# Keys and values of the second attention leave the first attention's loop; keys are repeated by transfers; the first expert group is routed beside group 2's transfers

## What is computed

```python
x = x + tanh(g_xattn[0]) * attention0(layernorm(x), ctx)   # one head, softmax(q ctx^T) ctx
x = x + tanh(g_ffn[0])   * moe0(layernorm(x))              # 16 experts, top 4, one shared expert
x = x + tanh(g_xattn[1]) * attention1(layernorm(x), ctx)   # 16 heads of 8, k = ctx Wk^T + bk, v = ctx Wv^T + bv
x = x + tanh(g_ffn[1])   * moe1(layernorm(x))              # 8 experts, top 2
# attention1:
q = query_states @ Wq.T + bq
k = key_value_states @ Wk.T + bk
v = key_value_states @ Wv.T + bv
attn = softmax(einsum('bhqd,bhkd->bhqk', q * SCALE, k))
out = einsum('bhqk,bhkd->bhqd', attn, v) @ Wo.T + bo
```

## Time and profile before

| | |
|---|---|
| time, median of 3 runs | 337.23 us (336.18 to 338.31) |
| profiled execution | 339.97 us, of which the span is 337.3 us |
| PE busy | 296.4 us (88% of the span), weight loads 222.8 us |
| DVE busy | 247.9 us (73%) |
| ACT, POOL busy | 165.1 us (49%), 103.8 us (31%) |
| mean granted TensorE clock | 0.969 of 2.4 GHz |
| chain that ended last | PE 54%, DVE 17%, ACT 8%, DMA 7%, issue 6% |

### The profile page before, as it was taken

One profiled execution on the slowest core, in us unless ns is written; L12 is line 12 of the kernel. 1 busy time (PEld: TensorE's weight loads), 2 busy tenths in 40 slices (PEclk: granted clock), 3 DMA queues, 4 the chain that ended last, 5 costly groups with the idle time before them and its releaser, 6 DMA issues.

```text
span 337.3 us, 5717 instructions
## 1 busy us (share of the span) xinstructions
PE 296.4 (88%) x1488; PEld 222.8 (66%) x1488; DVE 247.9 (73%) x727; ACT 165.1 (49%) x427; POOL 103.8 (31%) x157
## 2 busy tenths in 40 slices
PE   1889879998998999858898898898887999999995
PEld 1677756665766666537787787787874667676662
DVE  2479778976887977654868868868868877958662
ACT  1237653224233242466798797797862233233321
POOL 6216615020055010263529829829401010100000
PEclk9999958999899999987999999999999999999999
DMA  7901104818605125000000000000004233061550
GB/s 216 328 16 38 31 4 153 247 28 256 166 26 176 54 97 157 0 1 0 2 1 3 2 0 0 0 0 1 3 17 154 83 121 116 22 209 36 165 179 31
DMA packets 16279, 26.45 MB, mean 78 GB/s; under 512 B 2789, under 2 KB 5299, under 8 KB 16051
## 3 DMA queue, kind: packets, MB, share of 16 engines
q1 hardware_dynamic: 15448, 24.93, 24.0%
q10 hardware_dynamic: 808, 1.25, 1.3%
HBM read 24.29 MB, written 1.25 MB: 76 GB/s over the span
## 4 chain that ended last, share of the span: by engine, by line
PE 54%; DVE 17%; ACT 8%; DMA 7%; issue 6%; SPq 3%; POOL 2%; DVEq 1%; ACTq 0%; POOLq 0%
PE bank L547 20%; PE Ybank L569 13%; DMA CR<-comb_rows 4%; PE bank L722 4%; ACT PX L977 3%; DVE cmx L1327 2%; DVE xn L1088 2%; PE Tb L471 2%; DMA comb_rows<-ct 2%; DVE st L1074 2%; SPq L295 1%; DMA CB<-in_consts 1%; DVE recT L1343 1%; SPq L302 1%; DVE xl L1094 1%
## 5 line engine op out<-in xcount | busy, mean ns | idle before, releaser
L890 ACT ACTIVATE sg<-bank 128x512 f32<-128x512 f32 x64 | 38.1, 597 | 76.6 <-PE bank L547 59.4
L334 POOL TENSOR_TENSOR rstd<-ve,mhalf 128x4 f32<-128x4 f32 x16 | 16.2, 1011 | 162.2 <-DVE ve L1081 162.2
L1227 DVE TENSOR_TENSOR hb<-sg,CR 128x512 f32<-128x512 f32 x64 | 44.9, 703 | 18.4 <-DMA CR<-comb_rows 8.4
L1220 DVE TENSOR_TENSOR sg<-sg,bank 128x512 f32<-128x512 f32 x64 | 43.5, 680 | 6.7 <-PE bank L547 4.2
L1327 DVE TENSOR_REDUCE cmx<-bank 128x4 f32<-128x308 f32 x64 | 28.3, 472 | 17.5 <-PE bank L695 17.2
L342 POOL TENSOR_TENSOR KS<-kr,CB 128x1232 fp32r<-128x1232 f32 x16 | 36.1, 2260 | 11.3 <-PE bank L695 11.3
L547 PE MATMUL bank<-xh,WBH 128*128 128x512 f32 x68 | 36.2, 533 | 1.2 <-DVE sg L1220 0.6
L547 PE MATMUL bank<-xh,UPH 128*128 128x512 f32 x64 | 36.2, 566 | 0.0
L569 PE MATMUL Ybank<-hb,W2T 128*128 128x512 f32 x64 | 33.5, 604 | 3.1 <-DVE hb L1227 3.1
L569 PE MATMUL Ybank<-hb,downw 128*128 128x512 f32 x64 | 33.0, 599 | 0.4 <-DVE hb L1227 0.3
L977 ACT ACTIVATE PX<-bank,cmx 128x77 f32<-128x77 f32 x128 | 29.4, 355 | 0.0
(11 more groups left out here) (179 smaller groups left out, 612.0 us busy)
## 6 DMA issues: line engine op xcount, KB each, us to landing
CR<-comb_rows SPq DMA_DIRECT2D x64, 128.0 KB, 3.0
CR<-comb_rows SPq DMA_DIRECT2D x32, 256.0 KB, 3.4
VX<-in_vs_seed SPq DMA_DIRECT2D x4, 320.0 KB, 4.6
w13raw<-in_w SPq DMA_DIRECT2D x1, 1088.0 KB, 11.6
X<-in_x SPq DMA_DIRECT2D x4, 256.0 KB, 9.5
upraw<-in_up SPq DMA_DIRECT2D x4, 256.0 KB, 4.7
out_x<-X SPq DMA_DIRECT2D x4, 256.0 KB, 3.6
cT<-in_ctxT SPq DMA_DIRECT2D x4, 154.0 KB, 6.1
```

Source lines behind the costliest of these rows:

```text
L334: nc.gpsimd.tensor_tensor(rstd[:], ve[:], mhalf[:], ALU.pow).then_inc(rstd_rdy, 1)
L890: A(sg[:, k % 2, :], Gb[k % 2][:], ACT.Silu).then_inc(m.s_done, 1)
L1220: V.tensor_tensor(sg[:, k % 2, :], sg[:, k % 2, :], Ub[k % 2][:], ALU.mult).then_inc(m.t2, 1)
L1227: V.tensor_tensor(hb[:, k % 2, :], sg[:, k % 2, :], CR[:, k % RING, :], ALU.mult).then_inc(m.h_done, 1)
```

## The change

- Stage A: no key work, no value work, no `RK`. Norms 1 to 5 have buffers of their own (`mvA`, `rstdA` and so on), and ACT applies three of them (new `norm_apply` on ACT, four instructions each); the sum of probabilities comes from ACT's exponentials. `W4` and `CN` are loaded by SP.
- Between stage A and unit 0: values (PE, then ACT), keys (PE, `keys_hi` on ACT, `keys_lo` on DVE) for all four groups. The value bias goes through the output projection into `tgbo`.
- The repeating of the keys is done by 16 transfers, `kh` and `kl` to `kr`. They and the 24 value pieces are issued by `later_load`, three behind each unit from unit 14 to unit 27.
- The routing of group 0 is written to DRAM before SP waits for the end of stage A. Each group's routing is one transfer instead of four.
- POOL: `expand_keys` and `place_values(0)` stand behind the splits of `up` and ahead of norm 9.

The core of the diff:

```diff
-            sp.wait_ge(vs_zero, 1)
-            sp.wait_ge(v_done, NG)
-            for h, c, row, key, n in pieces:
-                sp.dma_start(VS[row:row + n, c, h % UH - chunk_head(c)], Vn[key:key + n, h]).then_inc(in_vs, 16)
+            def place_keys(n):
+                a, s = n // NHG, n % NHG
+                src = kh if a < 2 else kl
+                sp.dma_start(kr[32 * a:32 * (a + 1), s, :], src[32 * s:32 * (s + 1), :].bitcast(F32)).then_inc(in_kr, 16)
+
+            def place_values(n):
+                h, c, row, key, rows = pieces[n]
+                sp.dma_start(VS[row:row + rows, c, h % UH - chunk_head(c)], Vn[key:key + rows, h]).then_inc(in_vs, 16)
...
+                first, per = 10, 3
+                if n == first:
+                    sp.wait_ge(k_l, NG)
+                    sp.wait_ge(vs_zero, 1)
+                    sp.wait_ge(v_done, NG)
+                for i in range(per * (n - first), per * (n - first) + per):
+                    if 0 <= i < NHG * 4:
+                        place_keys(i)
+                    elif 0 <= i - NHG * 4 < len(pieces):
+                        place_values(i - NHG * 4)
...
-                for t in range(GB):
-                    sp.dma_start(at[0:m.E, t * P:(t + 1) * P], ct[32 * t:32 * t + m.E, :]).then_inc(rows_out, 16)
-                sp.wait_ge(rows_out, 16 * GB * (m.route_base + g + 1))
+                sp.dma_start(at[0:m.E, :].rearrange("e (t n) -> t e n", t=GB), ct[0:GB * m.E, :]).then_inc(rows_out, 16)
+                sp.wait_ge(rows_out, 16 * (m.route_base + g + 1))
+                if m is mB and g == 0:
+                    sp.wait_ge(a_pv, START + NG)
...
-            sp.wait_ge(a_pv, START + NG)
...
-            pool.wait_ge(d_set, 1)
-            pool.wait_ge(kr_done, START + NG * NHG)
-            expand_keys(0, 0, first=True)
-            expand_keys(1, 1, first=True)
             inv_std(NG + 3)
-            pool.wait_ge(in_seed, 64)
-            pool.wait_ge(in_vs, 16 * len(pieces))
-            place_values(0, 0, first=True)
             inv_std(NG + 4)
             pool.wait_ge(in_up, 96)
             for n in range(NG):
                 split_up(n)
+            pool.wait_ge(in_kr, 16 * NHG * 4)
+            expand_keys(0, 0, first=True)
+            expand_keys(1, 1, first=True)
+            pool.wait_ge(in_seed, 64)
+            pool.wait_ge(in_vs, 16 * len(pieces))
+            place_values(0, 0, first=True)
+            pool.wait_ge(bo_rdy, 1)
             inv_std(2 * NG + 1)
...
+            a_probs_T(2)
+            a_turn(5)
+            a_mix(2)
+            m_logits(mB, 0)
+            a_probs_T(3)
+            a_mix(3)
+
+            setup_values(0)
+            pe.wait_ge(a_exp, NG)
+            setup_values(1)
+            m_route_T(mB, 0)
+            setup_values(2)
+            setup_values(3)
+            pe.wait_ge(v_done, 1)
+            setup_keys(0)
+            pe.wait_ge(v_done, 2)
+            setup_keys(1)
...
+            m = mB
+            m_up(m, 0, 0, ring=False)
+            pe.wait_ge(x_done, START + NG)
+            setup_keys(2)
...
             m_up(m, 0, 1, ring=False)
-            pe.wait_ge(x_done, START + NG)
+            pe.wait_ge(k_l, 2)
+            setup_keys(3)
+            pe.wait_ge(k_l, NG)
             m_body(m, 0, (NG + 2, m, 1))
```

More of the change, by code:

```diff
@@ L263, in load_x, with load_cT @@
                 sp.dma_start(X[:, g * GT:(g + 1) * GT], x[:, g * GT:(g + 1) * GT]).then_inc(in_x[g], 16)
+            def load_cT(half):
+                cols = slice(half * 2 * GS, (half + 1) * 2 * GS)
+                sp.dma_start(cT[:, cols], ctxT[:, cols]).then_inc(in_ct[half], 16)
             load_x(0)
[L266 to L269, removed]
+            load_x(1)
@@ L846, in norm_hi, with norm_apply @@
                 A(dst, Tb[:], ACT.Copy).then_inc(xh_rdy, 1)
-            norm_hi(2, xf[:])
+            def norm_apply(n, g):
+                par = n % 2
+                act.wait_ge(rstdA_rdy, n)
+                act.wait_ge(xnT, n - 1)
+                for t in range(GB):
+                    i = A(xn[:, t * P:(t + 1) * P], X[:, g * GT + t * P:g * GT + (t + 1) * P], ACT.Identity,
+                          bias=shiftA[:, par, t:t + 1], scale=rstdA[:, par, t:t + 1])
+                i.then_inc(xn_rdy, 1)
             def a_exps(g):
@@ L940, in m_body @@
                         m_route_copy(nxt[1], nxt[2])
+            norm_hi(1, xf[:, 0])
+            act.wait_ge(in_w, 16)
+            A(WQH[:], W4[:, 0, :], ACT.Copy).then_inc(su_a, 1)
+            norm_hi(2, xf[:, 1])
             a_exps(0)
+            norm_apply(3, 2)
             a_probs(0)
-            with act.Fori(0, NG - 2) as g:
-                a_body(g, xf[:], True)
-            a_body(NG - 2, xh[:, 0:GT], True)
-            a_body(NG - 1, None, False)
+            norm_hi(3, xf[:, 0])
+            a_exps(1)
+            norm_apply(4, 3)
+            a_probs(1)
+            norm_hi(4, xf[:, 1])
+            a_exps(2)
+            norm_apply(5, 0)
+            a_probs(2)
+            norm_hi(5, xh[:, 0:GT])
+            a_exps(3)
+            m_route_act(mB, 0)
+            a_probs(3)
+            values(0)
+            values(1)
+            m_route_copy(mB, 0, first=True)
+            values(2)
+            values(3)
+            keys_hi(0)
+            keys_hi(1)
             m = mB
             m_silu(m, 0, 0)
+            keys_hi(2)
             m_silu(m, 0, 1)
+            keys_hi(3)
             m_body(m, 0, (NG + 2, m, 1), begun=2)
@@ L1105, in _, with norm_statsA @@
-            dve.wait_ge(in_x[0], 16)
-            norm_stats(1, 0)
-            norm_apply(1, 0, first=True)
-            dve.wait_ge(in_x[1], 16)
-            norm_stats(2, 1)
-            dve.wait_ge(in_small, 16)
-            values(0)
-            norm_apply(2, 1)
+            def norm_statsA(n, g):
+                par = n % 2
+                if n > 2:
+                    dve.wait_ge(xn_rdy, n - 2)
+                for t in range(GB):
+                    i = V.bn_stats(st[:, t, :], xt(g, t))
+                i.then_inc(statsA, 1)
+                wait_apart(dve, statsA, n)
+                for t in range(GB):
+                    i = V.bn_aggr(mvA[:, par, t, :], st[:, t, :])
+                i.then_inc(aggrA, 1)
+                wait_apart(dve, aggrA, n)
+                if n > 2:
+                    dve.wait_ge(rstdA_rdy, n - 2)
+                V.tensor_scalar(veA[:, par], mvA[:, par, :, 1], EPS, None, ALU.add)
+                V.tensor_scalar(lessA[:, par], mvA[:, par, :, 0], -1.0, None, ALU.mult).then_inc(varA, 1)
@@ L1292, in _ @@
             i.then_inc(gw_hi, 1)
-            dve.wait_ge(in_x[3], 16)
-            with dve.Fori(0, NG - 3) as g:
-                a_body(g, g + 2, True, g + 3)
+            a_update(0)
             dve.wait_ge(x_done, START + 1)
-            a_body(NG - 3, NG - 1, True, 0)
-            a_body(NG - 2, 0, True)
-            norm_lo(NG + 1, 0)
-            a_body(NG - 1, None, False)
+            norm_statsA(5, 0)
+            a_share(1)
+            a_maxima(2)
+            a_update(1)
+            a_share(2)
+            a_maxima(3)
+            dve.wait_ge(bv_mm, 1)
+            V.scalar_tensor_tensor(out=tgbo, in0=tgbo, scalar=tg[:, 1:2], in1=bank[0][:, 0:P], op0=ALU.mult,
+                                   op1=ALU.add).then_inc(bo_rdy, 1)
+            norm_lo(NG + 1, 0)
+            a_update(2)
+            route_add(mB, 0)
+            a_share(3)
+            route_vals(mB, 0)
+            route_top(mB, 0)
+            route_pick(mB, 0)
+            route_weights(mB, 0)
+            a_update(3)
             norm_stats(NG + 2, 1)
+            keys_lo(0)
+            keys_lo(1)
+            keys_lo(2)
             m = mB
```

325 lines of the change are left out of this document (153 added, 172 removed).

## The result

| | before | changed |
|---|---|---|
| time, median | 336.75 us (336.18 to 338.31, 4 runs) | 355.93 us (355.25 to 356.82, 4 runs) |
| ratio | 1 | 1.056 (1.052 to 1.061) |
| profiled execution | 339.97 us, span 337.3 us | 356.54 us, span 354.0 us |
| mean granted TensorE clock | 0.969 | 0.942 |

The changed kernel is 19.2 us slower. The forecast was 351.0 us, in a range of 342 to 358: the direction and the main mechanism held, the size was 4.9 us short. The page of the changed kernel: busy times, and in 40 slices the busy share of PE and the granted clock.

The account below looks back on a forecast made before the run. It took DVE's routing as the bound from stage A to B, and PE with short CR waits in stage B. Terms -4.5 - 1.9 - 1.3 + 19.5 + 2 = +13.8 us gave 351.0 us against the median, range 342 to 358.

Parts of the forecast that it names:

- stage A and what is given back: Stage A to unit 0: comb 9 us earlier, part lost to values and keys ahead of unit 0; -4.5 us.
- one transfer for the rows: Routing rows at group starts: one issue instead of four, -1.9 us in group 1 and -1.3 us in stage D.
- pieces and norm 9, to unit 24: Group 2 to unit 24: SP's queue becomes slowest, norm 9 waits on POOL for the last value piece; +19.5 us.
- behind the stop, to unit 29: PE after the stop: 15 to 20 matmuls at the low clock; +2 us, bounds 0 to 4.
- slower still: Rival: transfers get in each other's way in SP's queue, the stop grows by 6 us; 357 us, chance 0.12.
- At nothing: The two expand_keys on POOL, 4.48 us, move into group 2 where POOL idles; counted as no cost.
- The rule on setup: SP's issues: the skill's page suggests 0.35 us a piece, 15 us less from unit 16 on, time near 341 us.
- SP keeps pace: Rival: pieces cost SP 0.5 us, group 2 takes 2.6 us a unit; 341 us, chance 0.13.
- Faster: Rival: last piece lands just behind unit 23, stop under about 7 us; 333 or 328.5 us, chance 0.05.
- Hidden anyway: Rival: transfers are hidden and only stage A counts; needs norm 9 ahead of the wait, no chance of its own.

Follow-up runs that it names:

- no pieces: The changed kernel without its 40 key and value transfers, so the second attention reads zeros; 331.4 us, ratio 0.983 to the kernel before.
- norm first: The changed kernel with POOL computing norm 9 ahead of its waits for key and value pieces; 342.19 us, ratio 1.016 to the kernel before.
- four per unit: The changed kernel with four pieces behind a unit instead of three; 347.61 us, ratio 1.027 to the kernel before.
- new order: The kernel before with POOL's queue in the order of the changed one, pieces still landing in stage A; 337.07 us, ratio 1.000.
- spread: The changed kernel with norms 9 and 10 ahead of the value wait, one piece behind units 10 to 13, then two; 339.23 us, ratio 1.007 to before.
- POOL pieces: The changed kernel with norms 9 and 10 ahead of the value wait, value pieces issued by POOL, key pieces by SP; 333.50 us, ratio 0.988 to before.
- longer dummies: The changed kernel with 77 extra matmuls on PE, results unused, in the stop before norm 9; 351.42 us, ratio 1.038 to the kernel before.

## Why the prediction was right, and where it was short

The cleanest pair for the trace is the changed kernel beside "no pieces", the same program but for the pieces, at 1.0 us apart (unit 11) before the first of them. From there the difference grows to 21.0 at unit 24, 24.2 at unit 29, 24.8 at unit 32 and 25.4 at unit 63. With the 1.0 off:

| step | forecast | measured | from |
|---|---|---|---|
| stage A and what is given back | -4.5 | -4.1 | -5.6 of "no pieces" less the next row |
| one transfer for the rows | -3.2 | -1.5 | its own run |
| pieces and norm 9, to unit 24 | +19.5 | +20.0 | units 11 to 24 |
| behind the stop, to unit 29 | +2 | +3.2 | units 24 to 29 |
| from unit 29 on | 0 | +1.2 | units 29 to 63 |
| sum | +13.8 | +18.8 | whole: 355.93 - 336.75 = +19.2 |

**The largest step held, place and size.** The forecast let SP's queue set the stop, worked the clock forward to the last piece and through POOL's copies to DVE, and named "some 17 us": the trace has 17.02. A unit held SP 3.59 us in group 3 where 3.46 was forecast, and the value pieces agree with the earlier trace rows: median 785 ns against 749. Three experiments carry it: norm first, four per unit, and the unchanged time of the new order alone.

**Two prices in it were off, in opposite senses.** The key pieces have their own row now (source line of SP: ns min, median, max, first and last start):

```profile
L291 SPq DMA_DIRECT2D kr<-kh x8: 582/592/706, 77.2 to 90.3; - x8
L291 SPq DMA_DIRECT2D kr<-kl x8: 545/590/595, 91.0 to 99.8; - x8
L295 SPq DMA_DIRECT2D VS<-Vn x24: 551/785/887, 100.4 to 130.5; - x24
```

A key piece took 0.59 us, near the lower bound of 0.5, not the 0.78 taken: it moves 154 KB, far more than a value piece, and holds SP for less time. Against it, the routing rows of group 2 were late: issued at 84.63, their `CR` at 88.40, 3.8 us where the forecast had 1.5. Waits of SP by line (total, times, longest):

```profile
SPq L333 <- DMA comb_rows<-ct: 12.3, 8, 3.1
```

That longest wait is 3.1 us, where "no pieces" has at most 1.9: behind six key pieces in one queue the small write landed over a microsecond later. This is the mechanism of the rival "slower still", in one place and at 1.2 us instead of 6. The ten key pieces from unit 16 on cost 1.9 us less than was put down for them, the rows of group 2 cost 2.3 us more: that the step came out within 0.5 us is partly luck.

**At nothing, for a reason that did not hold: the expansions on POOL.** The forecast put them at nothing because POOL idles. POOL did, but DVE was stretched by some 4 us beside them, at unit 20. In the changed kernel that stayed without a cost, since SP set the pace; in "spread" and "POOL pieces", where it no longer does, it cost 2 us and more.

**Term mis-sized: one transfer for the routing rows, -3.2 against -1.5.** The step counted the landing from the start of the issue, and took 1.3 us from stage D by the length of its waits. In stage D some 0.5 us stayed, in the last group.

**Term mis-sized: the clock, +2 against 3.2.** The bound of 0 to 4 held. The longer dummies show 2.4 us of it as the granted clock; the rest, 0.8 us, was there with the clock up too, and was not taken apart.

**Left out: +1.2 us from unit 29 on.** Half of it, 0.6 us, is lost between units 32 and 39, where the granted clock of the changed kernel's trace is low (0.50) from 272.0 to 275.4 us and that of "no pieces" is not; the kernel before with one transfer has such a stretch too, without any stop, so it need not come from the change. The other 0.6 us, between units 29 and 32, stays open. The 1.9 us that the longer dummies give back there are no sign of the stop either: all traces have a low clock early in stage C, in the changed kernel from 166.1 to 173.0 us, before from 149.0 to 155.8, with no pieces from 140.8 to 147.6, but with the longer dummies only from 162.5 to 165.9. It is as short in "norm first", in the new order and in the kernel before with one transfer, and these gain 0.7 to 1.3 us on before in the same place. What makes it short in some executions is not shown.

**Stage A held**: -4.1 against -4.5, although its inner times did not. `comb` was ready at 35.0, not 37, and the first `hb` came at 46.18, not 49. Of the 9.75 us at unit 0, 7.5 are left at unit 7, and 5.8 when the changed kernel is laid beside the new order's execution instead of that of before; by the medians it is 4.1. The early part came out better than forecast and was given back behind it.

**The rule on setup.** SP's value pieces cost 0.785 us at the median, so the trace of the changed kernel speaks once more against the 50 ns and a few hundred ns of the Trainium skill, "SBUF — State Buffer", section "The DMA setup-cost knee". On POOL's queue twelve of them took 6.26 and 6.49 us, 0.53 us each, closer to that page and still above the 0.35 us estimated from it.

**The rivals.** "SP keeps pace" was wrong in time, but half of its ground was there: key pieces did cost little. Its 341 us is what norm first gave, 342.19, by another way. "Faster" needed a stop under 7 us; even at 3.31 us (four per unit) the kernel stayed slower than before, because the lateness had only moved into the units. So that condition was too weak: SP's time per unit had to fall under 2.75 us as well. Its sum is also off by one: 337.2 - 4.5 - 1.9 - 1.3 + 3.5 + 1 is 334.0, not 333 (and 329.5, not 328.5). Of the other sums one does not come out either, without weight: a first down projection at 51.5 instead of 56.7 leaves 5.2 us, not 5.4. "Hidden anyway" did need norm 9 ahead of the wait, and with it, alone, was not reached either.

## What to carry to other kernels

When transfers are moved behind a loop's iterations, add what they hold the issuing queue for to what an iteration already holds it for, and compare with the iteration: here 3.6 us against 2.75, and the last transfer landed 15 us after DVE had finished the unit ahead of the wait. Then look down the queue of every engine that waits for the last transfer, for an instruction that somebody else needs sooner: one power of 1.0 us behind that wait was worth 13.7 us. When work moves on an idle POOL, look also at what DVE does at that time: norm 9 took 1.12 us alone and 5.00 us beside two expansions. Make a sum against the profiled execution only after seeing how far that execution lies from the median, and take the gains from runs where it matters.

## What the runs showed of the hardware

- The time that a transfer between SBUF tiles holds SP's queue did not follow its size: 0.59 us for 154 KB over 32 partitions, 0.785 us at the median for a value piece of 1 to 77 rows (0.55 us for the two of one row), 0.58 us for the routing rows. The same value pieces held POOL's queue for 0.53 us each.
- A write of the routing rows that stood behind six key pieces in the same queue was waited for 3.1 us, against 1.9 us without the pieces.
- An instruction of DVE that ran beside one of POOL's `expand_keys` (2.24 to 2.74 us each) took about as long as that one: 2264 and 2195 ns instead of 186 and 225 (changed kernel), 2.40 us instead of 0.69 (`hb`, norm first), 2.61 us instead of 0.69 (`ql`, POOL pieces). Not every one did: `sg`, which reads one input from a PE result, kept its 0.67 to 0.69 us in the same stretches.
- Two executions of kernels with equal medians (336.99 and 337.07 us) had spans of 337.3 and 333.9 us, so up to 3 us between single executions need not be an edit's doing.
